# A fused two-layer kernel: how the Sinkhorn scaling starts and returns to logarithms, and where the last residual sums stand

## The chip, the cores and the metric

The kernel runs on one core of a Trainium2 chip. A core has five engines that run side by side and meet through semaphores: TensorE (PE: matrix products and transposes), VectorE (DVE), ScalarE (ACT: functions from tables), GpSimd (POOL) and SyncE (SP: starts most transfers). The metric is the device time of one execution in microseconds (us), lower is better.

## The reference, cut to what matters

Two layers work on x of 2 x 512 x 512. The change touches only the end of the second layer: the attention's residual sum, the layer norm after it, and the last block, in which each of the 1024 tokens has its own 4 x 4 matrix, made doubly stochastic by 50 scaling steps.

```python
x = x + ga * _L1_attn_ref(h, ...)
h = _layernorm(x, axis=-1) * (1 + cb) + sb
# last block, on h as x
x_norm = x * jax.lax.rsqrt(jnp.mean(x * x, axis=-1, keepdims=True) + RMS_EPS)
H_res_logits = (x_norm @ W_res.T).reshape(B, T, n, n) + H_res_base
Z = logits / tau                        # tau 0.1
def step(carry, _):                     # 50 times, u and v from zero
    u, v = carry
    u = -jax.nn.logsumexp(Z + v[..., None, :], axis=-1)
    v = -jax.nn.logsumexp(Z + u[..., :, None], axis=-2)
    return ((u, v), None)
H_res = jnp.exp(Z + u[..., :, None] + v[..., None, :])
H_pre = jax.nn.softmax(H_pre_logits, axis=-1)
H_post = jax.nn.softmax(H_post_logits, axis=-1)
H_res = (1.0 - g) * I + g * H_res
x_pre = jnp.einsum('btnc,btn->btc', x_streams, H_pre)
y = x_pre @ W_branch
x_mixed = jnp.einsum('btij,btjc->btic', H_res, x_streams)
y_distributed = jnp.einsum('btc,btn->btnc', y, H_post)
```

## The kernel before, in words

Every engine runs one straight program. `story` calls stages in one order for all five engines, and a stage adds instructions only to the engines whose class defines it; so the order on each engine is the order of the calls, and an engine that waits holds everything behind it. The 1024 tokens are eight tiles of 128 rows: tiles 0 to 3 are batch 0, tiles 4 to 7 batch 1. `acc[:, i]` holds x of tile i, `hh[b][:, i % 4]` its attention output and later its normed row.

`attentions` runs 16 rounds (Q), eight to a batch, each over four key tiles (kt): `scores_b` (PE, then exponentials on ACT), `pv` (PE), `out1` (ACT copies the sums) and `out2` (PE turns them, DVE divides and writes 2 x 32 columns of `hh`). `out2` of a round is called at kt 1 of the next one; that of the last round stands behind the loop. PSUM banks 4, 5 and 6 are taken in turn (`spin`), so a product can wait until an older one is read.

`head(E, b)` then takes the four tiles of a batch: `residual` (DVE multiplies `hh` by the modulation row `mt[1, 2, b]`, POOL adds it to `acc`), `moments` (DVE statistics, POOL power), `norm` (ACT), `scaled_rows` (DVE multiplies, POOL adds), `square` (ACT), `turn_l` (PE transposes, ACT copies), `rms`, and `logits` (PE, then DVE). Batch 0's head is spread over the second batch's rounds; batch 1's stands alone behind the loop, with a product `logits` of a tile ahead of the next tile's transposes.

`mix_y(1)` makes the two softmaxes of batch 1. Then `sinkhorn` works on all tiles at once, 128 columns a step. W holds logarithms, P = exp(W), T a scaled copy, m the sums, a and b their reciprocals. It takes maximum, difference, exponential, sum, logarithm and difference once along rows and once along columns, which is one of the 50 steps, and then 49 steps in blocks of 17, 16 and 16. A step is six DVE instructions: multiply by b, row sums, reciprocal a, multiply by a, column sums, reciprocal b; the first of a block has no multiply by b. Between blocks logarithms of a and b are added to W and P is made anew ("return to logarithms"). Beside it, `merged` puts `branch` (the product with W_branch) on ACT, POOL and PE, one of its pieces for each three or four calls of the scaling. `finish` mixes, and SP writes the output.

Lines used below: L1082 and L1700 residual, L1087 to L1092 and L1705 moments, L1442 norm, L1099 and L1713 scaled rows, L792 transposes, L803 logits product, L1225 its result, L1231 to L1273 scaling on DVE, L1563 exponential, L1568 logarithm, L1284 to L1288 softmax sums.

## Time and profile before

| | us |
|---|---|
| median of 3 runs | 1542.0 |
| lowest and highest | 1539.73 and 1542.78 |
| the profiled execution | 1540.01 |
| its span, first to last instruction | 1538.2 |

The profile is one execution, and durations come from it; 1.81 us of it lie around its span. Of the span PE is busy 82%, DVE 65%, POOL 48% and ACT 41%, but the last 185 us are another kernel than the rest: there PE has little to do and DVE most.

### The profile page before, as it was taken

What the parts mean: (1) busy time and instruction counts of PE and PEld (TensorE: products, weight loads), DVE (VectorE), ACT (ScalarE), POOL (GpSimd) and SP (SyncE); (2) the same over time, 40 slices, a digit from 0 to 9 for tenths busy, and PEclk for the clock granted to TensorE, in tenths of its full rate; (3) what the DMA queues carried; (4) which work ended last, traced back from release to release, by engine and by line L of the source; (5) the groups of instructions that cost most, each with busy time, mean ns of one, the idle gap of its engine ahead of it and who ended that gap; (6) DMA issues with size and microseconds to landing.
All of it is one profiled execution on the core that took longest, in us unless ns stands there. A gap on an engine that the chain in (4) does not pass through costs nothing. (4 is left out here: it accounts for less than half of the span.)

```text
span 1538.2 us, 18571 instructions
## 1 busy us (share of the span) xinstructions
PE 1260.4 (82%) x6079; PEld 890.4 (58%) x6079; DVE 1001.4 (65%) x1717; ACT 630.0 (41%) x1177; POOL 736.3 (48%) x742
## 2 busy tenths in 40 slices
PE   4889999999999999999999999777989999841000
PEld 2677767767767777777777777556843334330000
DVE  6836655656565666656556566675678887447888
ACT  2334333333433333333334333246227767733223
POOL 0456765665756656657657657665200011041007
PEclk9999999999999999999999999898959989955555
DMA  4211122122122112112112111210754200000001
GB/s 157 79 49 55 56 69 83 55 62 89 40 79 69 56 56 67 56 56 69 55 56 69 53 58 49 80 58 1 144 113 69 53 30 2 1 1 0 0 0 55
DMA packets 70552, 86.47 MB, mean 56 GB/s; under 512 B 6853, under 2 KB 40805, under 8 KB 69882
## 3 DMA queue, kind: packets, MB, share of 16 engines
q1 hardware_dynamic: 68586, 82.57, 19.8%
q10 hardware_dynamic: 1872, 2.72, 0.5%
q8 instruction: 50, 0.82, 0.2%
q14 instruction: 44, 0.36, 0.1%
HBM read 77.49 MB, written 7.51 MB: 55 GB/s over the span
## 5 line engine op out<-in xcount | busy, mean ns | idle before, releaser
L1183 DVE TENSOR_REDUCE nm<-banks 128x2 f32<-128x1024 f32 x128 | 152.2, 1221 | 33.4 <-PE banks L742 32.9
L1425 ACT ACTIVATE yTh<-yF 128x512 fp32r<-128x512 f32 x64 | 40.4, 632 | 318.9 <-DVE yF L1035 318.9
L1637 POOL TENSOR_TENSOR sw<-sw,sinT 128x512 f32<-128x512 f32 x80 | 103.3, 1291 | 137.8 <-ACT sw L1376 137.8
L1651 POOL TENSOR_TENSOR dec<-gb,gcol 128x512 f32<-128x512 f32 x64 | 70.8, 1107 | 195.3 <-DVE Sd L1001 191.2
L1531 ACT ACTIVATE Pb<-banks 128x512 f32<-128x512 f32 x256 | 135.0, 602 | 52.8 <-PE banks L763 52.4
L540 PE MATMUL banks<-hTh,wgh 128*128 128x512 f32 x256 | 122.1, 477 | 0.0
L973 DVE SCALAR_TENSOR_TENSOR gs<-tg,banks 128x512 f32<-128x512 f32 x64 | 44.0, 688 | 118.4 <-ACT tg L1383 118.4
L592 PE MATMUL banks<-st,qt 128*128 128x128 f32 x384 | 80.7, 294 | 37.1 <-DVE Sd L1001 21.1
L620 PE MATMUL banks<-woh,yTh 128*128 128x512 f32 x256 | 104.6, 409 | 3.5 <-DVE yTl L1038 3.5
L540 PE MATMUL banks<-hTh,wqh 128*128 128x512 f32 x256 | 106.3, 415 | 0.0
L620 PE MATMUL banks<-woh,yTl 128*128 128x512 f32 x256 | 101.7, 397 | 0.0
L620 PE MATMUL banks<-wol,yTh 128*128 128x512 f32 x256 | 101.0, 394 | 0.0
L540 PE MATMUL banks<-hTh,wql 128*128 128x512 f32 x256 | 100.7, 394 | 0.0
L540 PE MATMUL banks<-hTh,wgl 128*128 128x512 f32 x256 | 100.7, 393 | 0.0
L540 PE MATMUL banks<-hTl,wgh 128*128 128x512 f32 x256 | 100.7, 393 | 0.0
L540 PE MATMUL banks<-hTl,wqh 128*128 128x512 f32 x256 | 99.9, 390 | 0.0
L1700 POOL TENSOR_TENSOR acc<-acc,hh 128x512 f32<-128x512 f32 x8 | 10.5, 1313 | 184.3 <-DVE hh L1082 184.3
L763 PE MATMUL banks<-qsT,ksT 50*128 50x512 f32 x256 | 92.9, 503 | 7.1 <-DVE hh L1207 4.5
L1038 DVE TENSOR_TENSOR yTl<-yF,yTh 128x512 fp32r<-128x512 f32 x64 | 68.7, 1073 | 44.7 <-ACT yTh L1425 44.7
L593 PE MATMUL banks<-xc,Sd 128*128 128x128 f32 x512 | 95.9, 286 | 0.0
L592 PEld LDWEIGHTS banks<-st,qt 128*128 128x128 f32 x384 | 64.9, 205 | 46.2 <-DVE Sd L1001 24.4
L1642 POOL TENSOR_TENSOR qT<-tt,sw 128x512 f32<-128x512 f32 x64 | 83.1, 1298 | 14.6 <-DVE tt L968 6.5
(307 smaller groups left out, 3378.3 us busy)
## 6 DMA issues: line engine op xcount, KB each, us to landing
gb<-g_scr SPq DMA_DIRECT2D x64, 256.0 KB, 3.3
raw<-in_wmod SPq DMA_DIRECT2D x40, 256.0 KB, 2.7
raw<-in_wg SPq DMA_DIRECT2D x32, 256.0 KB, 2.7
raw<-in_wo SPq DMA_DIRECT2D x32, 256.0 KB, 2.8
raw<-in_wq SPq DMA_DIRECT2D x30, 256.0 KB, 2.6
qsT<-q_scr SPq DMA_DIRECT2D x24, 256.0 KB, 6.6
q_scr<-hl SPq DMA_DIRECT2D x32, 128.0 KB, 4.3
mt<-mods_scr SPq DMA_DIRECT2D x12, 256.0 KB, 4.8
```

The lines of the kernel that those rows point to most:

```text
L540: mm = pe.matmul(banks[bk][:, :], w_[:, k, :], x_[:, k, b * 512:(b + 1) * 512], start=(c == 0), stop=(c == 11))
L592: pe.matmul(o, qt[:, h, :], st[:, h, :], start=True, stop=False)
L593: mm = pe.matmul(o, Sd[:, h, :], xc[:, h, :], start=(n == 0), stop=True)
L620: mm = pe.matmul(banks[bO][:, :], y_[:, h, :], w_[:, :], start=(c == 0), stop=(c == 11))
L763: pe.matmul(banks[bk], k_[64 * g:64 * g + 50, p // 4, kt * 128:(kt + 1) * 128], q_[64 * g:64 * g + 50, p % 8, :], start=True, stop=True).t ...
L973: ve.scalar_tensor_tensor(out=gs[t % 2][:, n, :], in0=tg[:, :], scalar=1.0, in1=banks[bk][:, :], op0=ALU.add, op1=ALU.mult).then_inc(*v_ga ...
L1038: ve.tensor_tensor(yTl[:, :, :], yF[:, :, :], yTh[:, :, :].bitcast(F32), ALU.subtract).then_inc(*v_yl.up(s))
L1183: ve.tensor_reduce(nm[:, b, i, p:32:16], pairs[z_][:, :].rearrange("p (g t) -> p g t", g=2), AX.X, ALU.max, negate=True).then_inc(*v_nm.up ...
L1531: ac.activation(Pb[kt % 2][:, 2 * g + pr, :], banks[bk], ACTF.Exp, scale=0.25).then_inc(*a_exp.up(b, qd, kt, pr, g))
L1637: po.tensor_tensor(s_[:, :], s_[:, :], sinT[:, :], ALU.mult).then_inc(*g_rope.up("sin", kind, t, n))
L1642: po.tensor_tensor(dst, tt1[j][:, :], s_[:, :], ALU.add).then_inc(*g_rope.up("add", kind, t, n))
L1651: po.tensor_tensor(dec[:, :, :], gb[s % 2][:, :, :], bc(gcol[:, t % 2, heads(t), n], 2, 128), ALU.subtract).then_inc(*g_dec.up("sub", s))
```

## The change

It has three parts.

1. The scaling begins from W with the rows' and then the columns' maxima taken off, with no logarithm. T = exp of W without row maxima gives the first row sums, P = exp of W without both gives all that follows. 25 steps, one return to logarithms, 25 steps. The step's order is unchanged.
2. The softmaxes of batch 1 (`mix_y`, in two parts) stand inside the return, and the branch of batch 0 runs beside the first half, that of batch 1 beside the second.
3. In the last round `out2` of the round before is called at kt 0 instead of kt 1, and columns 0 to 223 of each half of tiles 4 to 7 are multiplied (DVE) and added (POOL) there (`residual_most`). Behind the loop only 2 x 32 columns a tile are left, done for all four tiles by two DVE instructions (`residual_last`). `last_head` replaces the head of batch 1: all moments, then all scaled rows (the additions of tiles 5 and 7 on DVE), then squares and transposes, with a tile's transposes ahead of the product of the tile before.

```diff
+    def most(t):
+        return t.rearrange("p (g c) -> p g c", g=2)[:, :, 0:224]
+    def last(t):
+        return t.rearrange("p i (g c) -> p i g c", g=2)[:, :, :, 224:256]
...
+        def residual_most(self, i):
+            ve, b = self.e, i // 4
+            h_ = most(hh[b][:, i % 4, :])
+            ve.wait_ge(*v_out("o", b, 6))
+            ve.wait_ge(*d_mt[2, b](1))
+            ve.tensor_tensor(h_, h_, most(mt[1, 2, b][:, :]), ALU.mult).then_inc(*v_res.up("most", i))
+        def residual_last(self, b):
+            ve, a_, h_ = self.e, last(acc[:, 4 * b:4 * b + 4, :]), last(hh[b][:, :, :])
+            m_ = mt[1, 2, b][:, :].rearrange("p (g c) -> p g c", g=2)[:, :, 224:256]
+            ve.wait_ge(*v_out("o", b, 7))
+            ve.tensor_tensor(h_, h_, bc(m_, 1, 4), ALU.mult).then_inc(*v_res.up("last", b))
+            ve.wait_ge(*v_res("last", b))
+            ve.tensor_tensor(a_, a_, h_, ALU.add).then_inc(*v_res.up("sum", b))
...
         def moments(self, of, i):
             ve = self.e
+            if of == "h" and i >= 4:
+                ve.wait_ge(*v_res("sum", 1))
             ve.wait_ge(*g_x(of, i))
...
+            if i in (5, 7):
+                ve.wait_ge(*v_ln("h", "c", i))
+                ve.wait_ge(*d_mt[3, b](1))
+                ve.tensor_tensor(h_, h_, mt[1, 3, b][:, :], ALU.add).then_inc(*v_ln.up("h", "d", i))
...
+        def residual_most(self, i):
+            po, b = self.e, i // 4
+            a_ = most(acc[:, i, :])
+            po.wait_ge(*v_res("most", i))
+            po.tensor_tensor(a_, a_, most(hh[b][:, i % 4, :]), ALU.add).then_inc(*g_x.up("h", i))
...
+    def last_head(E):
+        E.residual_last(1)
+        for i in range(4, 8):
+            E.moments("h", i), E.norm("h", i)
+        for i in range(4, 8):
+            E.scaled_rows(i)
+        for i in range(4, 8):
+            E.square(i)
+            E.turn_l(i, E.spin())
+            E.rms(i)
+            if i > 4:
+                E.logits(i - 1, E.spin())
+        E.logits(7, E.spin())
...
-    def sinkhorn(E):
...
+    def scaling_steps(E, c, k, n, first):
+        for it in range(n):
+            if it:
+                E.sk_mul(c, k + 1, c.T, c.bv, True), (yield)
+                E.sk_sum(c, k + 2, c.T, False, v_sk("sk", k + 1)), (yield)
+                E.sk_inv(c, k + 3, c.av), (yield)
+                k += 3
+            E.sk_mul(c, k + 1, c.T, c.av, False, None if it else first), (yield)
+            E.sk_sum(c, k + 2, c.T, True, v_sk("sk", k + 1)), (yield)
+            E.sk_inv(c, k + 3, c.bv), (yield)
+            k += 3
+    def first_half(E):
+        c = Sink
+        E.sk_scale(c, 0), (yield)
+        E.sk_max(c, 1, False, v_sk("sk", 0)), (yield)
+        E.sk_sub(c, 2, False), (yield)
+        E.sk_exp(c, 3, c.T), (yield)
+        E.sk_max(c, 4, True, v_sk("sk", 2)), (yield)
+        E.sk_sub(c, 5, True, 3), (yield)
+        E.sk_exp(c, 6, c.P), (yield)
+        E.sk_sum(c, 7, c.T, False, a_sk("sk", 3), v_sk("sk", 5)), (yield)
+        E.sk_inv(c, 8, c.av), (yield)
+        yield from scaling_steps(E, c, 8, 25, 6)
+        k = KMID
+        E.sk_ln(c, k + 1, c.av, v_sk("sk", k - 2)), (yield)
+        E.sk_ln(c, k + 2, c.bv, v_sk("sk", k)), (yield)
+        E.mix_y(1, 0)
+        E.sk_add(c, k + 3, c.av, False, a_sk("sk", k + 1)), (yield)
+        E.sk_add(c, k + 4, c.bv, True, v_sk("sk", k + 3), a_sk("sk", k + 2)), (yield)
+        E.sk_exp(c, k + 5, c.P), E.mix_y(1, 1), (yield)
+    def second_half(E):
+        c, k = Sink, KMID + 5
+        E.sk_sum(c, k + 1, c.P, False, a_sk("sk", k)), (yield)
+        E.sk_inv(c, k + 2, c.av), (yield)
+        yield from scaling_steps(E, c, k + 2, 25, None)
+        for part in range(3):
+            E.sk_h(c, k + 2 + 3 * 49 + 1 + part, part), (yield)
...
-                if kt == 1 and Q:
+                if kt == (1 if Q < 15 else 0) and Q:
                     E.out2(*before(b, qd), E.spin())
+                if Q == 15 and kt < 2:
+                    E.residual_most(4 + 2 * kt), E.residual_most(5 + 2 * kt)
...
-        stream(E, head, 1).rest()
-        E.mix_y(1)
-        merged(stream(E, sinkhorn), joined(stream(E, branch, 0), stream(E, branch, 1))).rest()
+        last_head(E)
+        merged(stream(E, first_half), stream(E, branch, 0)).rest()
+        merged(stream(E, second_half), stream(E, branch, 1)).rest()
```

Three places show how instructions stand. First PE, from the last round's products of probabilities and values (Pb) to the logits products (rwt); `cst,oS` is out2, `cst,hh` the transposes. Before:

```order
L783 MATMUL banks<-cst,oS 128x128 x4
L763 MATMUL banks<-qsT_218,ksT_212 128x512 x4
L773 MATMUL banks<-Pb_243,vp_214 32x512 x4
L773 MATMUL banks<-Pb_244,vp_214 32x512 x4
L783 MATMUL banks<-cst,oS 128x128 x4
L792 MATMUL banks<-cst,hh_166 128x128 x4
L803 MATMUL banks<-rwt,hT_248 128x24 x4
L792 MATMUL banks<-cst,hh_166 128x128 x4
L803 MATMUL banks<-rwt,hT_248 128x24 x4
L792 MATMUL banks<-cst,hh_166 128x128 x4
```

After, in the same place:

```order
L794 MATMUL banks<-cst,oS 128x128 x4
L774 MATMUL banks<-qsT_218,ksT_212 128x512 x4
L784 MATMUL banks<-Pb_244,vp_214 32x512 x4
L774 MATMUL banks<-qsT_218,ksT_212 128x512 x4
L784 MATMUL banks<-Pb_243,vp_214 32x512 x4
L784 MATMUL banks<-Pb_244,vp_214 32x512 x4
L794 MATMUL banks<-cst,oS 128x128 x4
L803 MATMUL banks<-cst,hh_166 128x128 x8
L814 MATMUL banks<-rwt,hT_248 128x24 x4
L803 MATMUL banks<-cst,hh_166 128x128 x4
L814 MATMUL banks<-rwt,hT_248 128x24 x4
L803 MATMUL banks<-cst,hh_166 128x128 x4
```

The first out2 moved one group of scores and one of values up, and two tiles' transposes now stand ahead of the first logits product.

Second DVE, from the out2 of the last round (`rd` and `hh<-banks,rd`) on. Before:

```order
L1203 RECIPROCAL rd<-banks 128x16
L1207 TENSOR_TENSOR hh_166<-banks,rd 128x4x32 x2
L1082 TENSOR_TENSOR hh_166<-hh_166,mt_253 128x512 x2
L1087 BN_STATS bst<-acc 128x6
L1089 BN_AGGR mv<-bst 128x2
L1091 TENSOR_SCALAR nmean<-mv 128x1
L1092 TENSOR_SCALAR ve<-mv 128x1
L1082 TENSOR_TENSOR hh_166<-hh_166,mt_253 128x512
```

After, from one out2 earlier:

```order
L1235 RECIPROCAL rd<-banks 128x16
L1239 TENSOR_TENSOR hh_166<-banks,rd 128x4x32 x2
L1100 TENSOR_TENSOR hh_166<-hh_166,mt_253 128x2x224 x4
L1235 RECIPROCAL rd<-banks 128x16
L1239 TENSOR_TENSOR hh_166<-banks,rd 128x4x32 x2
L1106 TENSOR_TENSOR hh_166<-hh_166,mt_253 128x8x32
L1108 TENSOR_TENSOR acc<-acc,hh_166 128x8x32
L1115 BN_STATS bst<-acc 128x6
L1117 BN_AGGR mv<-bst 128x2
L1119 TENSOR_SCALAR nmean<-mv 128x1
L1120 TENSOR_SCALAR ve<-mv 128x1
```

Four multiplications went ahead of the last out2, and two of 256 columns stand between it and the first statistics.

Third ACT, at a return to logarithms: the logarithms of a and b, the exponential P, table loads, and pieces of the branch (`yb`, `prod`). The first return before:

```order
L1568 ACT_TABLE_LOAD
L1568 ACTIVATE a<-a 128x32
L1604 ACTIVATE banks<-yb_270,hp 128x128
L1568 ACTIVATE b<-b 128x32
L1563 ACT_TABLE_LOAD
L1563 ACTIVATE P<-W 128x128
```

The only return after:

```order
L1608 ACT_TABLE_LOAD
L1608 ACTIVATE a<-a 128x32
L1608 ACTIVATE b<-b 128x32
L1646 ACTIVATE mx_264<-yb_272,hp 128x128
L1615 ACT_TABLE_LOAD
L1615 ACTIVATE hp<-hp 128x32
L1603 ACTIVATE P<-W 128x128
```

The softmax exponential (hp) came in ahead of P. From the end of attention on, ACT's program held eight table loads, and now holds these two.

## Rows read from the trace of the kernel before

**Rows 1.** Busy time by stage: stretch, length, busy us (instructions) per engine, clock, DMA.

```profile
1353.30:1365.10 11.80, 0.00 (x0) 0.00 (x0) 10.28 (x25) 2.44 (x3) 9.90 (x12) 0.57 0.01 1
1365.10:1381.80 16.70, 11.48 (x48) 9.76 (x48) 3.21 (x11) 5.76 (x13) 7.41 (x9) 0.50 0.00 1
...
1391.60:1500.00 108.40, 7.35 (x23) 4.83 (x23) 95.15 (x291) 27.93 (x86) 8.59 (x14) 0.50 0.00 0
```

**Rows 2.** Timeline, end of attention: start, us, engine, line, [idle before <- releaser].

```profile
1348.30 0.26 DVE L1203 RECIPROCAL rd<-banks 128x16 f32<-128x16 f32 x1 [11.85 <-PE banks L783]
...
1354.14 1.29 DVE L1082 TENSOR_TENSOR hh<-hh,mt 128x512 f32<-128x512 f32 x2
...
1356.59 0.69 DVE L1087 BATCH_NORM_STATS2 bst<-acc 128x6 f32<-128x512 f32 x1 [1.15 <-POOL acc L1700]
```

**Rows 3.** Timeline, head of batch 1: moments, norm, scaled rows.

```profile
1358.26 0.69 DVE L1087 BATCH_NORM_STATS2 bst<-acc 128x6 f32<-128x512 f32 x1
...
1359.27 0.14 DVE L1092 TENSOR_SCALAR ve<-mv 128x1 f32<-128x1 f32 x1
...
1360.20 0.99 POOL L1705 TENSOR_TENSOR rs<-ve,neghalf 128x1 f32<-128x1 f32 x1
...
1361.49 0.81 ACT L1442 ACTIVATE hh<-acc,nmr,rs 128x512 f32<-128x512 f32 x1 [1.62 <-POOL nmr L1707]
...
1363.84 1.26 POOL L1713 TENSOR_TENSOR hh<-hh,mt 128x512 f32<-128x512 f32 x1
```

**Rows 4.** Timeline, transposes and logits products of batch 1.

```profile
1365.15 1.12 PE L792 MATMUL banks<-cst,hh 128*128 128x128 f32 x4 [11.87 <-POOL hh L1713]
...
1372.64 1.90 PE L803 MATMUL banks<-rwt,hT 128*128 128x24 f32 x8 [0.69 <-ACT hT L1558]
...
1374.37 1.09 PE L792 MATMUL banks<-cst,hh 128*128 128x128 f32 x4
...
1379.66 1.90 PE L803 MATMUL banks<-rwt,hT 128*128 128x24 f32 x8 [0.69 <-ACT hT L1558]
1381.60 0.24 DVE L1225 SCALAR_TENSOR_TENSOR lg<-banks,r,rbc 128x24 f32<-128x24 f32 x1 [3.20 <-PE banks L803]
```

**Rows 5.** Timeline, from the softmax sums to the first block of scaling.

```profile
1382.58 0.19 DVE L1284 TENSOR_REDUCE hs<-hp 128x8 f32<-128x32 f32 x1 [0.30 <-ACT hp L1573]
...
1383.15 0.22 DVE L1231 TENSOR_SCALAR W<-lg 128x128 f32<-128x128 f32 x1
...
1384.05 0.31 ACT L1563 ACTIVATE T<-W 128x128 f32<-128x128 f32 x1 [1.21 <-DVE W L1246]
...
1386.50 1.28 ACT L1563 ACT_TABLE_LOAD   x1
...
1387.80 0.31 ACT L1563 ACTIVATE T<-W 128x128 f32<-128x128 f32 x1
...
1391.59 0.29 DVE L1241 TENSOR_REDUCE m<-P 128x32 f32<-128x128 f32 x1 [1.33 <-ACT P L1563]
```

**Rows 6.** Timeline, the two returns to logarithms.

```profile
1428.36 0.23 ACT L1568 ACTIVATE a<-a 128x32 f32<-128x32 f32 x1 [23.48 <-DVE b L1251]
...
1430.65 0.28 DVE L1241 TENSOR_REDUCE m<-P 128x32 f32<-128x128 f32 x1 [1.00 <-ACT P L1563]
...
1465.06 0.23 ACT L1568 ACTIVATE a<-a 128x32 f32<-128x32 f32 x1 [22.58 <-DVE b L1251]
...
1467.36 0.29 DVE L1241 TENSOR_REDUCE m<-P 128x32 f32<-128x128 f32 x1 [1.29 <-ACT P L1563]
```

**Rows 7.** Groups on DVE, 1391.6 to 1501.7: count | busy, mean ns | idle before.

```profile
L1241 DVE TENSOR_REDUCE m<-T 128x32 f32<-128x128 f32 x95 | 31.5, 332 | 3.2
...
L1256 DVE TENSOR_TENSOR T<-P,a 128x128 f32<-128x128 f32 x49 | 14.6, 298 | 1.7
```

**Rows 8.** Busy time in two stretches of the last round, columns as in Rows 1.

```profile
1346.00:1348.00 2.00, 2.00 (x12) 0.71 (x4) 0.00 (x0) 0.07 (x1) 0.00 (x0) 0.50 0.00 0
1348.00:1350.00 2.00, 1.55 (x10) 0.71 (x12) 0.75 (x3) 1.27 (x3) 0.00 (x0) 0.95 0.00 0
```

91 lines of the change are left out of this document (38 added, 53 removed).

## The prediction

> **What bounds the kernel now.** I read the busy time by stage first, then the timeline of the last 185 us, because the change leaves all before the last attention round as it is. The reader is to see a serial tail. From 1353.3 to 1365.1 DVE and POOL work in turn and PE does nothing; from 1365.1 to 1381.8 PE works at the low clock; from 1391.6 to 1500 DVE is busy 95.15 of 108.4 us [rows 1], and what is not busy there are the gaps between dependent small instructions and the two returns. So each us taken off this chain is a us of the kernel, as long as the replacement is on the same chain. `finish`, behind it, is the same code and starts when the scaled matrix H is there.
>
> **Part 1, residual sums beside the last round.** DVE has been idle for 11.85 us when it divides the second last round's sums [rows 2], so four multiplications of 448 columns fit. A 512-column one takes 0.65 us (1.29 for two) [rows 2], so about 0.6 each, 2.4 in all; POOL's additions, of which the 512-column kind takes 1.26 [rows 3], are at most 1.26 each, 5.0 in all. Even taken strictly one after another that is 7.4 us. They can start when the moved out2 has been divided, which I put some 4 us ahead of 1348.30, the time of its division now [rows 2], since it moves one key tile up and then waits for nothing that is late. They end at about 1352, ahead of the last out2's DVE work (up to 1354.14) [rows 2]. So they cost nothing; without that cover they would cost what they cost now. Moving out2 from kt 1 to kt 0 moves four transposes and one wait for a bank from one key tile to the one before; the sum of PE's work in the round stays, and I take 0, with bounds of -1 and +1 us, as the idle of ACT and PE around out2 may split otherwise.
>
> Now the first multiplication starts at 1354.14 and the first statistics at 1356.59, waiting for POOL [rows 2]: 2.45 us. After, two DVE instructions of 256 columns stand there. Between 0.29 us for 128 columns [rows 5] and 0.65 for 512, that is 0.42 each, with gaps 0.9. First statistics at 1355.05.
>
> **Part 2, moments and scaled rows.** A tile's moments take 1359.27 - 1358.26 plus 0.06, 1.07 us [rows 3]; the four now run back to back: the fourth is ready at 1359.3. POOL's power to ACT's norm is 1360.20 to 1361.49, 1.29 us from the power's start, which is 0.2 behind the DVE result, and powers follow each other each 1.2. Powers then start at 1356.3, 1357.5, 1358.7 and 1359.9, POOL is through at about 1361.1, and the norms start at 1357.5 to 1361.15 and take 0.81 each [rows 3]. DVE multiplies tile 4's row from 1359.35, well ahead of POOL. **POOL's first scaled row** can only start when its four powers are done, at 1361.1; with the 0.4 us that DVE may hold it up, and 1.26 for itself [rows 3], tile 4 is ready at 1362.75 where it now is at 1365.1 (the first transposes start at 1365.15 [rows 4]). Tile 5 needs no POOL and is ready by 1361.5 to 1362.7. Tiles 6 and 7, with POOL and DVE in turn, are ready at 1365.2 and 1365.8.
>
> **Part 3, transposes and logits.** Now a tile costs 3.51 us ((1379.66 - 1372.64) / 2 [rows 4]): product 1.90, transposes that end 0.92 behind the product's end (1374.37 + 1.09 - 1372.64 - 1.90), then the copy on ACT, for which PE waits. With the next tile's transposes ahead of the product that wait is covered. After, PE does T4 1.12, T5 0.94, L4 1.90, T6 0.94, L5 1.90, T7 0.94, L6 1.90, L7, and the result starts 1.94 behind L7's start (1381.60 - 1379.66 [rows 4]): 11.6 us. T6 is due at 1366.7 and T7 at 1369.6, behind their rows, so nothing else is late. The last logits come at 1362.75 + 11.6 = 1374.3 instead of 1381.60. **Parts 1 to 3 give 7.3 us.**
>
> **Part 4, the start of the scaling.** Now from the last logits (1381.60) to the first sum of P (1391.59) it is 9.99 us [rows 5]: the softmax of batch 1, then two rounds of exponential and logarithm with four table loads of 1.28 in DVE's way. After, 0.27 to the scale as the softmax has it now, scale 0.25, maximum, difference, maximum, difference at 0.33 to 0.37 each (reductions 0.332 + 3.2 / 95 = 0.366, 128-column products 0.298 + 1.7 / 49 = 0.333 [rows 7]), and the first sum starts 1.9 us behind the last logits. The exponential T (0.31, start 0.9 behind the scale [rows 5]) is done before the second difference asks for it, P is done before the first multiply. Saved: 8.1.
>
> **Part 5, the steps.** Sixteen steps less one multiply take 1465.06 - 1430.65 = 34.41 us [rows 6]; with 0.33 for the multiply a step is (34.41 + 0.33) / 16 = 2.17. There were 49 in three blocks and are 50 in two: one step more and one left-out multiply fewer, 2.5 us lost. The branch brings the same POOL instructions as before, so the same disturbance is in the step.
>
> **Part 6, the return.** Now 1428.36 to 1430.65 and 1465.06 to 1467.36, 2.29 and 2.30 [rows 6]. After, the logarithm of a runs beside the last sum and reciprocal. Behind the reciprocal of b: logarithm of b, one branch piece on ACT (starts at 0.12, ends at 0.51), the table load 1.28, the softmax's exponential at 1.80, P right behind it, done at 2.27. DVE fits the softmax's difference and both additions into the load. But it has the softmax's sums, reciprocal and product in front of the next sum: they start at 2.06 and take 0.57 (1383.15 - 1382.58 [rows 5]). So 2.63, once. Saved: 4.59 - 2.63 = 2.0. If the softmax did not wait, it would be 2.3.
>
> A load and the exponential behind it start 1.30 us apart (1386.50 to 1387.80 [rows 5]), so a switch costs here the load and nothing more. The Trainium skill (ScalarE: Activation LUTs, What ACT_TABLE_LOAD costs) adds a drain of about 1.38 us to a load of 1.28; the trace doesn't show it. By the page the return would be some 1.4 longer.
>
> **The sum.** 7.3 + 8.08 - 2.5 + 1.96 = 14.8. The profiled execution took 1540.01 us, and would take 1525.2. It is 2.0 us under the median of the runs shown, 1542.0, near the lowest; so against the median, which is what I forecast, 1542.0 - 14.8 = **1527.2**.
>
> **Rivals.** (a) **PE's clock comes back in the head.** The granted clock is 0.50, the 1.2 GHz level, from 1365.1 to 1381.8, with PE busy 11.48 of 16.7 us [rows 1]. In the last round it was at 0.50 with PE busy 2.00 of 2.00 and at 0.95 in the next 2 us [rows 8]. After, PE works nearly without a break for 11 us. If the clock rose some 4 us in, the remaining 7.6 us would halve at most, 3.8, but ACT's copies then bind: I take 3, so 1524.2. Against it: the stage before it leaves PE idle for 9 us, and it starts low. The Trainium skill (TensorE: Matmul & The Clock Gate, Part 1) says that activity releases the throttle, and so speaks for this rival; what the stage shows so far, the low clock at two thirds busy, does not decide it. Chance 0.2.
>
> (b) **The head saves less.** POOL now runs four powers before any scaled row, and DVE and POOL take turns on their two-input instructions. If rows 4, 6 and 7 come each one POOL instruction and a DVE one later than I worked out (1.26 + 0.65), and the residual sums of the last round end 1 us late, 3 us are lost: 1530.2. For it: the bst row waited 1.15 us for POOL [rows 2]. Against: the four additions have 6 us of room. Chance 0.13.
>
> (c) **Slower: the step gets longer.** 298 small instructions decide the scaling. If the branch, which ACT can now run through at once instead of stopping at logarithms (it waited 23.48 and 22.58 us there [rows 6]), pressed POOL's instructions into DVE's, each step would pay. From 14.8 / 50 = 0.3 us a step on, the kernel is no faster; at 0.4 it is 5 us slower, 1547. For it, only that a product shows 0.298 mean where an undisturbed one is 0.29 [rows 7]. Against it: POOL has 14 instructions in 108 us, 8.59 us busy [rows 1]; even if each stopped DVE for its whole length it were 8.6. Chance 0.03.
>
> (d) **The last round pays what was moved into it**: out2 at kt 0 holds back the scores by a bank, or the DVE products delay the last out2. If the round ends later by what the residuals took, 2.4 us and more, the time is 1530. It is the case in which the change does not do what it says. Chance 0.06.
>
> **How the numbers follow.** My forecast has 0.5, (a) 0.2, (b) 0.13, (c) 0.03, (d) 0.06, and 0.08 is for a gain a little larger or smaller by causes not named. The forecast's own spread is the 1 us of part 1, 1 us of the head and the 1.5 us that the runs differ by. The range reaches down to (a) with 2 us of room and up past (b): 1522 to 1531.5. What a measurement can tell is about 0.2%, 3 us. Faster by more than that holds in all but (c): 0.96; within it 0.02; slower 0.02.
>
> **What would show it.** The four products of 2 x 224 columns and POOL's four additions all before the last out2, with DVE idle after; the first statistics 1.4 us behind the last `hh` product; first transposes 9 us, not 12, behind the last out2; L to L each 2.84 us at 0.50; the last logits 7.3 us nearer to the last out2; first sum of T 1.9 us behind them; the return 2.6 us; 50 steps of 2.17. The stretch behind the last `hh` product would be 14.8 us shorter, `finish` as long as now. Wrong would be: a clock of 1.00 in the head, POOL's first scaled row later than 8 us behind the last out2, or a step over 2.2.

## The result and the profile after

The changed kernel takes 1520.87 us (median of 4 runs, 1519.26 to 1522.55), the kernel before beside it 1540.87 (4 runs, 1538.23 to 1542.78): a ratio of 0.9872, 95% interval 0.9852 to 0.9891. That is 20.0 us less where 14.8 were forecast, and 1.1 us below the range. The profiled execution took 1520.73, its span is 1518.9.

First the busy time by stage of the kernel after (stretch, length, then busy us and instructions of PE, weight load, DVE, ACT, POOL, then the granted clock, DMA share and GB/s): from the second last to the last division of sums, from there to the first transposes, the head up to the last logits, and the two halves of the scaling. The third row answers to the row of before from 1365.10 on [rows 1].

```profile
1342.75:1350.37 7.62, 5.97 (x36) 1.81 (x36) 4.88 (x8) 4.73 (x9) 5.51 (x4) 1.00 0.00 0
1350.37:1359.01 8.64, 0.01 (x1) 0.01 (x1) 8.19 (x24) 3.28 (x5) 4.54 (x9) 0.69 0.01 2
1359.01:1369.36 10.35, 10.31 (x48) 9.95 (x48) 4.30 (x12) 5.21 (x13) 3.78 (x5) 0.50 0.01 2
1371.36:1425.80 54.44, 3.92 (x12) 2.50 (x12) 49.35 (x150) 12.26 (x41) 4.72 (x8) 0.50 0.00 0
1428.46:1482.42 53.96, 3.91 (x12) 2.50 (x12) 48.84 (x150) 11.53 (x40) 4.79 (x8) 0.50 0.00 0
```

PE now works through the head without a break, 10.31 of 10.35 us, where it was busy 11.48 of 16.70, and its clock stays at 0.50.

Cutting both traces at the same events gives the balance. The second last and last divisions (L1203 before, L1235 after), first statistics, first transposes, last logits (L1225, L1257), the first sum of the loop and the first product of the finish (H) are starts of instructions:

| stage | before | after | difference | forecast |
|---|---|---|---|---|
| start of the program to the third last division | 1335.67 | 1334.26 | -1.41 | 0 |
| two rounds' divisions, third last to last | 17.66 | 16.11 | -1.55 | 0 |
| last division to first statistics | 3.26 | 1.73 | -1.53 | -1.54 |
| to the first transposes | 8.56 | 6.91 | -1.65 | -0.9 |
| to the last logits | 16.45 | 10.35 | -6.10 | -4.9 |
| to the first product of H | 120.07 | 113.06 | -7.01 | -7.54 |
| to the end | 36.53 | 36.48 | -0.05 | 0 |
| sum | 1538.2 | 1518.9 | -19.3 | -14.8 |

The third row and those below it, with the second, are the changed part: 17.9 us. The first row is code that the change does not touch.

The end of attention and the head on DVE, kernel after (start, us, engine, line, instruction, in brackets the idle time before and what ended it); it answers to [rows 2] and [rows 3]:

```profile
1342.75 0.26 DVE L1235 RECIPROCAL rd<-banks 128x16 f32<-128x16 f32 x1 [7.71 <-PE banks L794]
...
1343.57 4.13 DVE L1100 TENSOR_TENSOR hh<-hh,mt 128x448 f32<-128x448 f32 x4
1350.37 0.26 DVE L1235 RECIPROCAL rd<-banks 128x16 f32<-128x16 f32 x1 [2.67 <-PE banks L794]
...
1351.18 0.42 DVE L1106 TENSOR_TENSOR hh<-hh,mt 128x256 f32<-128x256 f32 x1
1351.64 0.42 DVE L1108 TENSOR_TENSOR acc<-acc,hh 128x256 f32<-128x256 f32 x1
1352.10 0.69 DVE L1115 BATCH_NORM_STATS2 bst<-acc 128x6 f32<-128x512 f32 x1
...
1357.70 1.80 DVE L1131 TENSOR_TENSOR hh<-hh,mt 128x512 f32<-128x512 f32 x1
```

The four moved multiplications end at 1347.70 and DVE then waits 2.67 us for PE, so they cost nothing. POOL in the same kernel:

```profile
1344.27 5.51 POOL L1748 TENSOR_TENSOR acc<-acc,hh 128x448 f32<-128x448 f32 x4 [36.11 <-DVE hh L1100]
1353.34 0.55 POOL L1753 TENSOR_TENSOR rs<-ve,neghalf 128x1 f32<-128x1 f32 x1 [3.56 <-DVE ve L1120]
...
1356.54 0.93 POOL L1753 TENSOR_TENSOR rs<-ve,neghalf 128x1 f32<-128x1 f32 x1 [0.25 <-DVE ve L1120]
...
1357.69 1.26 POOL L1763 TENSOR_TENSOR hh<-hh,mt 128x512 f32<-128x512 f32 x1
```

Its additions end at 1349.78, 0.6 us before the last division. Three of the four powers take 0.55 us and not 0.99, and the first scaled row ends at 1358.95; the transposes start 0.06 later. PE in the head, which answers to [rows 4]:

```profile
1359.01 1.97 PE L803 MATMUL banks<-cst,hh 128*128 128x128 f32 x8 [8.67 <-POOL hh L1763]
1360.81 1.90 PE L814 MATMUL banks<-rwt,hT 128*128 128x24 f32 x8
1362.53 1.09 PE L803 MATMUL banks<-cst,hh 128*128 128x128 f32 x4
1363.42 1.74 PE L814 MATMUL banks<-rwt,hT 128*128 128x24 f32 x8
1364.99 1.09 PE L803 MATMUL banks<-cst,hh 128*128 128x128 f32 x4
1365.87 3.45 PE L814 MATMUL banks<-rwt,hT 128*128 128x24 f32 x16
```

No row but the first has a wait in brackets; before, the first product waited 2.86 us for ACT's copy and each of the other three 0.69. The start of the scaling and the one return, DVE and ACT, which answer to [rows 5] and [rows 6]:

```profile
1369.36 0.24 DVE L1257 SCALAR_TENSOR_TENSOR lg<-banks,r,rbc 128x24 f32<-128x24 f32 x1 [1.46 <-PE banks L814]
...
1371.36 0.29 DVE L1274 TENSOR_REDUCE m<-T 128x32 f32<-128x128 f32 x1
...
1425.80 0.23 ACT L1608 ACTIVATE b<-b 128x32 f32<-128x32 f32 x1 [0.57 <-DVE b L1286]
...
1426.34 1.28 ACT L1615 ACT_TABLE_LOAD   x1
1427.63 0.23 ACT L1615 ACTIVATE hp<-hp 128x32 f32<-128x32 f32 x1
...
1427.89 0.19 DVE L1324 TENSOR_REDUCE hs<-hp 128x8 f32<-128x32 f32 x1 [1.33 <-ACT hp L1615]
...
1428.46 0.28 DVE L1274 TENSOR_REDUCE m<-P 128x32 f32<-128x128 f32 x1
```

The first sum comes 2.00 us behind the last logits (1.9 forecast), the return takes 2.66 (2.63 forecast), and DVE's only wait in it is 1.33 us for the exponential behind the table load.

### The profile page after: what moved, and what is told of

Its sections match the earlier page's. It is cut to its first block and busy times, and to the rows that moved or that the text cites. A ratio compares the mean times of both kernels' runs of the same rounds, so it can differ in the third digit from the quotient of the medians.

```text
span 1518.9 us, 18570 instructions
## 1 busy us (share of the span) xinstructions
PE 1256.9 (83%) x6079; PEld 888.5 (58%) x6079; DVE 1006.9 (66%) x1722; ACT 621.5 (41%) x1165; POOL 732.3 (48%) x740
## 5 line engine op out<-in xcount | busy, mean ns | idle before, releaser
L979 DVE TENSOR_TENSOR tt<-banks,cosT 128x512 f32<-128x512 f32 x80 | 55.3, 691 | 53.1 <-ACT sw L1416 52.3
```

## The experiments

The theories: the gain is a sum of separate pieces on one serial chain (last round, head, start of the scaling, return), each of a size that can be read by undoing it alone. Against it stood that the last round's 1.55 us and the 1.41 us ahead of it were chance of the clock, that the head's surplus came from somewhere else than POOL and PE, and that a piece pays back elsewhere. "After" means the changed kernel. Stage lengths are cut as in the table above. Where a kernel was run once, only the stage lengths of its trace are read, not its time: wherever kernels share the code of a stage, these lengths agree within 0.05 us up to the first product of H.

### The two halves of the change

**before_again**: the kernel before, unchanged, as a measure of what a comparison can tell.

> The kernel before, unchanged, timed and profiled once more as a control. What it tells is how far two executions of the same program stand apart. Theory A (the low-clock stretch in the last attention round, 1344.8 to 1349 in the trace of before, is a property of the old order of that round): it is there again, the last round (division of out2 of the second last round to that of the last) takes 17.6 us, and the time is 1540.9. Rival B (the clock's low stretches fall where they fall, different in each execution): the last round takes 16.1 or 17.6 by chance, the list of low stretches differs from that of the first trace in one or two entries of some 4 us, each worth 1.4 to 1.6 us, and the runs spread over 3 to 4 us.

Measured: 1538.38 us (10 runs) beside 1538.54 (19 runs), ratio 1.0006 (0.9991 to 1.0021). Its two rounds take 17.68, head 28.27, last logits to H 120.04, each within 0.03 of the first trace. Its third last division is at 1332.99, 2.7 us earlier than in the first trace of the same code: the part ahead of the last rounds is where executions differ.

**scaling_only**: the new scaling behind the old last round and head.

```diff
-        last_head(E)
+        stream(E, head, 1).rest()
...
-                if kt == (1 if Q < 15 else 0) and Q:
+                if kt == 1 and Q:
-                if Q == 15 and kt < 2:
-                    E.residual_most(4 + 2 * kt), E.residual_most(5 + 2 * kt)
```

> Only the scaling part of the change (start with maxima, one return, softmax of batch 1 in it, branches split over the two halves); last round and head as before. From the two traces the scaling part is worth 8.0 (start) + 1.9 (return) - 2.9 (steps) = 7.0 us: 1533.9. If the parts were not additive, because the head's end meets the branch differently, it would be 1 us or more away. Under rival B the last round shows 16.1 or 17.6 us by chance, under theory A 17.6.

Measured: 1532.84 us, ratio 0.9953 (0.9936 to 0.9971), 5.7 us by the medians. Two rounds 17.64, head 28.29, last logits to H 113.04. The scaling's 7.0 us of the trace are there without the rest.

**head_only**: the new last round and head in front of the old scaling (49 steps behind the logarithms, softmaxes ahead).

```diff
-        merged(stream(E, first_half), stream(E, branch, 0)).rest()
-        merged(stream(E, second_half), stream(E, branch, 1)).rest()
+        E.mix_y(1, 0), E.mix_y(1, 1)
+        merged(stream(E, sinkhorn), joined(stream(E, branch, 0), stream(E, branch, 1))).rest()
```

> Only the head part of the change (out2 earlier in the last round, residual sums beside it, new head of batch 1); scaling with two returns and its old start. Head stage (last out2's division to the last logits) 19.0 us instead of 28.3: 9.3 gained, against 7.3 in the prediction. Theory A: 9.3 + 1.55 = 10.9 gained, 1530.0, last round 16.1 us. Rival B: 9.3 gained on average, 1531.6, last round 16.1 or 17.6. Rival C (the extra 2 us of the head came only with the new scaling behind it): 1533.6.

Measured: 1528.81 us, ratio 0.9935 (0.9913 to 0.9956). Two rounds 16.12, head 18.98, last logits to H 120.05. 9.7 us by the medians, 10.85 by the trace. With scaling_only the stages add up to 17.9 us, the changed part's whole gain: the halves do not disturb one another.

### The last round

**out2_late**: out2 stays at kt 1, the moved residual sums at kt 1 and 2.

```diff
-                if kt == (1 if Q < 15 else 0) and Q:
+                if kt == 1 and Q:
                     E.out2(*before(b, qd), E.spin())
-                if Q == 15 and kt < 2:
-                    E.residual_most(4 + 2 * kt), E.residual_most(5 + 2 * kt)
+                if Q == 15 and kt in (1, 2):
+                    E.residual_most(2 + 2 * kt), E.residual_most(3 + 2 * kt)
```

> The changed kernel, but out2 of the second last round stays at kt 1, and the residual products and sums follow at kt 1 and 2 instead of 0 and 1. The four sums then end some 2 to 3 us later, at about the time of the last out2's division; tile 4 and 5 are there, tiles 6 and 7 are asked for 2 and 3 us later. Theory A: the last round has its low-clock stretch again and takes 17.6 us, and the time is 1522.4 to 1523. Rival B: no difference beyond 0.5 us, 1521. If POOL's sums came too late, the head stage would be longer than 19.0 by up to 2 us.

Measured: 1524.20 us, ratio 0.9908 (0.9886 to 0.9930). Two rounds 17.67, as in the kernel before, and the head 19.80 instead of 18.99. DVE of out2_late:

```profile
1348.08 4.12 DVE L1100 TENSOR_TENSOR hh<-hh,mt 128x448 f32<-128x448 f32 x4
1352.29 0.26 DVE L1235 RECIPROCAL rd<-banks 128x16 f32<-128x16 f32 x1
...
1353.56 1.23 DVE L1108 TENSOR_TENSOR acc<-acc,hh 128x256 f32<-128x256 f32 x1
```

Now the multiplications end just ahead of the last division, POOL's four additions (5.73 us from 1348.78) run to 1354.51, and the addition of 256 columns on DVE takes 1.23 us instead of 0.42: that is the head's 0.8. The round's 1.56 us are apart from it.

**out2_alone** and **out2_alone_again**: the kernel before with nothing but the call moved.

```diff
-                if kt == 1 and Q:
+                if kt == (1 if Q < 15 else 0) and Q:
                     E.out2(*before(b, qd), E.spin())
```

> The kernel before with one call moved: in the last round out2 stands at kt 0 instead of 1; no residual sums in the round, old head, old scaling. If out2's place alone keeps the clock up in the last round, the two divisions around it add up to 16.1 us instead of 17.7 and no low stretch lies in the round: 1.5 us under before. If the residual products beside it were needed, or the new head, it is 17.6 to 17.7 with the low stretch, and the time is that of before. The head stage is the old one, 28.3 us, either way.

> The kernel before with one call moved (in the last round out2 at kt 0 instead of 1), once more for its trace: nine timed executions of it gave 1536.7 to 1541.1 us where before gave 1535.9 to 1542.7 beside it, which decides nothing on 1.5 us. Theory A (out2's place alone keeps the clock up): no low stretch in the last round, the two divisions around it add up to 16.1 us. Rival: the stretch is there as in before and it is 17.7; then the products and additions beside the round, or what they hold up, keep it away in the changed kernel.

Measured: out2_alone 1538.06 us, ratio 0.9998 (0.9985 to 1.0010), that is from 2.3 us less to 1.5 us more. The execution of it that was profiled took 2580.27 us, so its stages can't be set beside the others'. out2_alone_again took 1539.02 beside 1539.09, and its trace has two rounds of 16.11, head 28.27, last logits to H 120.03. So the call alone makes the round 1.55 us shorter; a timing of this size can neither show nor exclude it. PE, first of the kernel before:

```profile
1344.65 0.70 PE L763 MATMUL banks<-qsT,ksT 50*128 50x512 f32 x1 [0.45 <-ACT Pb L1531]
1345.28 1.93 PE L773 MATMUL banks<-Pb,vp 128*32 128x512 f32 x8
1347.15 1.12 PE L783 MATMUL banks<-cst,oS 128*128 128x128 f32 x4
```

and of out2_alone_again, where the same kinds of products stand at other times:

```profile
1343.09 1.06 PE L773 MATMUL banks<-Pb,vp 128*32 128x512 f32 x8
1344.09 0.66 PE L783 MATMUL banks<-cst,oS 128*128 128x128 f32 x4
...
1348.46 0.50 PE L763 MATMUL banks<-qsT,ksT 50*128 50x512 f32 x1 [0.45 <-ACT Pb L1531]
```

Eight products of probabilities and values 1.93 against 1.06, out2's transposes 1.12 against 0.66, a score 0.70 against 0.50: 1.53 us together, the 1.55 of the round. The granted clock says why. Kernel before, then out2_alone_again, 4 us each, from 9.3 and 9.0 us behind the third last division:

```profile
1345.00:1349.00 4.00, 3.69 (x15) 1.10 (x14) 0.66 (x3) 1.34 (x4) 0.00 (x0) 0.60 0.00 0
```
```profile
1345.29:1349.29 4.00, 3.22 (x18) 1.16 (x22) 0.27 (x2) 3.47 (x8) 0.00 (x0) 1.00 0.00 0
```

0.60 and 1.00. The kernel before has a stretch at 0.50 that begins 9.1 us behind the third last division, in both of its traces (1344.8 to 1348.2, and 1342.1 to 1345.5), and so have scaling_only (1350.1 to 1353.5) and out2_late (1343.7 to 1347.1). None of the twelve traces with the call at kt 0 has it, and all twelve have two rounds of 16.1.

**out2_later**: the call at kt 2, residual sums at kt 2 and 3.

```diff
-                if kt == (1 if Q < 15 else 0) and Q:
+                if kt == (1 if Q < 15 else 2) and Q:
...
-                if Q == 15 and kt < 2:
-                    E.residual_most(4 + 2 * kt), E.residual_most(5 + 2 * kt)
+                if Q == 15 and kt > 1:
+                    E.residual_most(2 * kt), E.residual_most(1 + 2 * kt)
```

> The changed kernel with the last round's out2 at kt 2, and the residual products and sums at kt 2 and 3. If each later place is as bad as kt 1, the low stretch is there and the last round takes 17.7 us; if kt 1 is only an unlucky place, the stretch is away and it takes 16.1. Beside that POOL's four sums end some 3 us later than in out2_late, behind the last out2: the head stage, 19.8 there, would be 22 to 23.

Measured (one run): 1530.40 us; two rounds 21.53 and head 19.90, where 17.7 or 16.1 and 22 to 23 were expected. A stretch of its last round, then DVE and PE at its end:

```profile
1350.00:1352.00 2.00, 1.74 (x6) 0.49 (x9) 0.00 (x0) 1.97 (x4) 0.00 (x0) 0.50 0.00 0
```
```profile
1355.10 4.10 DVE L1100 TENSOR_TENSOR hh<-hh,mt 128x448 f32<-128x448 f32 x4
...
1356.83 1.12 PE L794 MATMUL banks<-cst,oS 128*128 128x128 f32 x4 [0.72 <-ACT oS L1578]
...
1359.13 0.25 DVE L1235 RECIPROCAL rd<-banks 128x16 f32<-128x16 f32 x1
```

The low clock now lasts from 1346.7 to the end of the round, and the two rounds take 5.4 us more than after. Not all of that is the clock. Out2's division starts 1.16 us behind its transposes at the low clock (1353.13 to 1354.29 for the out2 before it), which for the last one would be 1357.99; it starts at 1359.13, because DVE is on the moved multiplications (1355.10 to 1359.20). So some 1.1 us belong to the multiplications and some 4.3 to the clock: the place of four transposes within a round of equal work decides between 16.1, 17.7 and about 20.4 us.

Why the clock falls in the one order and not in the other is not settled by these runs. In two stretches of 2 us, from 5.1 to 1.1 us ahead of the fall, PE was busy 1.83 and 1.63 us in the kernel before and 1.83 and 1.62 in out2_alone_again, and ACT alike. The last 1.1 us are where they part, kernel before, then out2_alone_again:

```profile
1343.70:1344.80 1.10, 0.65 (x4) 0.21 (x2) 0.00 (x0) 0.80 (x2) 0.00 (x0) 0.99 0.00 0
```
```profile
1344.30:1345.40 1.10, 0.88 (x6) 0.39 (x4) 0.58 (x3) 0.19 (x1) 0.00 (x0) 1.00 0.00 0
```

In the second, out2's transposes stand there. All five traces with a fall have PE busy 0.65 of these 1.1 us, all twelve without have 0.88 or 0.89. That goes with the fall; no run varies this alone, so it is not shown to be its cause.

### Inside the head

**product_first**: a tile's product ahead of the next tile's transposes, as before.

```diff
             E.square(i)
+            if i > 4:
+                E.logits(i - 1, E.spin())
             E.turn_l(i, E.spin())
             E.rms(i)
-            if i > 4:
-                E.logits(i - 1, E.spin())
```

> The changed kernel with the old order of products in the head alone: a tile's logits product ahead of the next tile's transposes. Head stage split: division to first statistics 1.73, statistics to first transposes 6.9, as in the trace of after. First transposes to last logits: 16.4 us as before (10.4 in after), if the order alone is worth the 6.1 us; 12 to 14 if a part of it came from rows being ready earlier. The forecast priced that order at 4.9 us (16.45 against 11.6).

Measured (one run): 1525.95 us; first transposes as after (+6.89 behind the statistics), from there to the last logits 14.27 instead of 10.35, head 22.90. PE of product_first:

```profile
1365.60 1.90 PE L814 MATMUL banks<-rwt,hT 128*128 128x24 f32 x8 [0.69 <-ACT hT L1598]
1367.33 1.09 PE L803 MATMUL banks<-cst,hh 128*128 128x128 f32 x4
1369.11 1.90 PE L814 MATMUL banks<-rwt,hT 128*128 128x24 f32 x8 [0.69 <-ACT hT L1598]
```

The old pitch of 3.51 us a tile is back, with the old wait. The order on PE alone is worth 3.9 us, of the head's 9.3 the largest piece. The other 2.2 of this stage's 6.1 us came with the rows of the tiles: the first product waited 2.86 us for its copy before, and 0.69 here.

**rows_on_pool**: all four additions of the scaled rows on POOL.

```diff
-            if i in (5, 7):
-                ve.wait_ge(*v_ln("h", "c", i))
-                ve.wait_ge(*d_mt[3, b](1))
-                ve.tensor_tensor(h_, h_, mt[1, 3, b][:, :], ALU.add).then_inc(*v_ln.up("h", "d", i))
```

> The changed kernel with all four additions of the scaled rows on POOL, as before. If POOL's additions bind: four of 1.26 plus waits behind DVE, tile 7's row some 1.5 to 2.5 us later than in after (1361.8 to 1362.4 there), still ahead of the time at which PE asks for it (1365). Then nothing is lost: head 19.0 to 19.3. If the move to DVE was what made the head faster than forecast, the head is 20 to 21 us.

Measured (one run): 1523.36 us; first transposes +7.35 (after: +6.91), to the last logits 10.97, head 20.05. The division of the additions between two engines is worth 1.06 us.

**sums_behind**: all residual sums behind the last round again, `residual` of tiles 4 to 7 in a row, the rest of the new head kept.

```diff
-        E.residual_last(1)
+        for i in range(4, 8):
+            E.residual("h", i)
...
-                if Q == 15 and kt < 2:
-                    E.residual_most(4 + 2 * kt), E.residual_most(5 + 2 * kt)
```

> The changed kernel without residual sums in the last round: out2 stays early, but all four 512-column products and additions stand behind the last out2. DVE does four products (2.6 to 4 us), POOL four additions of 1.26 in a row, tile 4's first. Statistics start 3.2 us behind the division as before instead of 1.73, and each of the next ones waits for POOL (1.3 each instead of 1.07), and POOL's powers stand behind the additions: first transposes some 3.5 us later than in after, head 22 to 23 us. By theory A the last round keeps the high clock (16.1 us from division to division), since only out2's place decides; if the products in it did, it is 17.6.

Measured (one run): 1529.65 us; two rounds 16.10, so the round is as short without the sums in it as with them: they are truly hidden. First statistics +5.37 instead of +1.73, first transposes +8.05, head 23.78. The hidden sums are worth 4.8 us in this head, three times the 1.5 us by which the first statistics came sooner than in the kernel before: there the sums stood between one tile's moments and the next, here all four would stand ahead of the first.

### The start of the scaling and the return

**no_return**: 50 steps in a row from the same start, with the softmaxes ahead of the scaling, where they used to stand.

```diff
         yield from scaling_steps(E, c, 8, 25, 6)
-        k = KMID
-        E.sk_ln(c, k + 1, c.av, v_sk("sk", k - 2)), (yield)
-        E.sk_ln(c, k + 2, c.bv, v_sk("sk", k)), (yield)
-        E.mix_y(1, 0)
-        E.sk_add(c, k + 3, c.av, False, a_sk("sk", k + 1)), (yield)
-        E.sk_add(c, k + 4, c.bv, True, v_sk("sk", k + 3), a_sk("sk", k + 2)), (yield)
-        E.sk_exp(c, k + 5, c.P), E.mix_y(1, 1), (yield)
...
+        E.mix_y(1, 0), E.mix_y(1, 1)
```

> The changed kernel with no return to logarithms at all: 50 steps in a row, the softmax of batch 1 ahead of the scaling as before the change. The result has the same definition, only a and b span more. From last logits to H: 113.06 less 2.66 (the return) plus 0.33 (one multiply by b) plus 1.2 (the softmax back on DVE's way, 1.28 from its first to its last instruction before) less 0: 111.9. If table load and logarithms had not been on the way, it would be 113.1 or more.

**softmax_ahead**: the return kept, the softmaxes ahead of the scaling.

```diff
-        E.mix_y(1, 0)
...
-        E.sk_exp(c, k + 5, c.P), E.mix_y(1, 1), (yield)
+        E.sk_exp(c, k + 5, c.P), (yield)
...
+        E.mix_y(1, 0), E.mix_y(1, 1)
```

> The changed kernel with the softmax of batch 1 back ahead of the scaling and the one return kept. Start: last logits to first sum 3.27 instead of 2.00. Return: without the softmax's exponential and its three DVE instructions behind the load, the first sum stands behind P alone: 2.66 becomes 2.27 (load, then P at 1.80, read at 2.13), or 2.1. So last logits to H 113.06 + 1.27 - 0.4 to 0.55 = 113.8 to 113.9. If the return hid the softmax wholly, it would be 114.3.

Measured (one run each): no_return 1522.15 us, last logits to H 111.77, so without the return H comes 1.29 us sooner than in after; softmax_ahead 1526.27, 113.59, which is 0.2 to 0.3 under what was expected; after 113.06. ACT and DVE of softmax_ahead at its return:

```profile
1432.04 0.23 ACT L1608 ACTIVATE b<-b 128x32 f32<-128x32 f32 x1 [0.57 <-DVE b L1286]
...
1434.21 0.28 DVE L1274 TENSOR_REDUCE m<-P 128x32 f32<-128x128 f32 x1 [1.55 <-ACT P L1603]
```

The bare return is 2.17 us and spares one multiply of 0.33, 1.84 net; the difference of the two kernels, 113.59 - 111.77 = 1.82, says the same. Putting the softmaxes into it makes it 0.49 longer and the start 1.26 shorter (first sum 3.26 behind the last logits in both kernels, 2.00 after), which should give 0.77; last logits to H gives 0.53. The rest is in the steps and was not followed. The prediction's aside that the return would be 2.3 without the softmax was 0.13 too long.

### What binds the head next

**after_again**: the changed kernel once more, as a neighbour for early_rows.

> The changed kernel, unchanged, as a control beside the next two. If the clock's dip in the last round goes with out2's old place, its last round is 16.1 us without a low stretch again, head 19.0, last logits to H 113.1, and the time is 20 us under before on the same chip, give or take 1.5 us by the low stretches ahead of the last round, which differ from one execution to the next.

Measured: 1522.01 us (4 runs) beside 1539.65 (7 runs), ratio 0.9884 (0.9866 to 0.9902); two rounds 16.11, head 18.99, last logits to H 113.07. Its third last division stands at 1335.80, so here the untouched part ahead is 0.13 us later than in the first trace of before, not 1.41 earlier. The interval holds the 17.9 us of the changed part (0.9884 x 1539.65 is 17.9 less).

**early_rows**: additions of tiles 4 and 5 on DVE (those of 6 and 7 on POOL), and both rows ahead of tile 7's moments, so that the first transposes no longer wait for POOL's four powers and its scaled row.

```diff
-            if i in (5, 7):
+            if i in (4, 5):
...
-        for i in range(4, 8):
+        for i in range(4, 7):
             E.moments("h", i), E.norm("h", i)
-        for i in range(4, 8):
-            E.scaled_rows(i)
+        E.scaled_rows(4), E.scaled_rows(5)
+        E.moments("h", 7), E.norm("h", 7)
+        E.scaled_rows(6), E.scaled_rows(7)
```

> The changed kernel with one more step in the head: tiles 4 and 5 are scaled whole on DVE (product and addition) ahead of tile 7's moments, tiles 6 and 7 have their addition on POOL. By the trace of after, tile 4's row waits 2.7 us for POOL to get through four powers. If that wait is what starts the transposes, they start 2.0 to 2.4 us earlier (4.6 us behind the first statistics instead of 6.9); the wait for tile 6 gives back up to 1 us, so the head is 17.5 to 18 us and the time 1 to 1.5 us under the changed kernel. If the head were bound by PE's own chain from the statistics on, no change.

Measured: 1524.44 us, ratio 0.9899 (0.9881 to 0.9916). The transposes start 2.24 us earlier (+4.67), but the last logits come 14.16 behind them: head 20.56, 1.6 more than after where 1 to 1.5 less was expected. PE and ACT of early_rows:

```profile
1357.71 1.11 PE L803 MATMUL banks<-cst,hh 128*128 128x128 f32 x4 [6.44 <-DVE hh L1131]
...
1363.32 1.90 PE L814 MATMUL banks<-rwt,hT 128*128 128x24 f32 x8 [3.17 <-ACT hT L1598]
```
```profile
1361.36 0.81 ACT L1482 ACTIVATE hh<-acc,nmr,rs 128x512 f32<-128x512 f32 x1 [2.81 <-POOL nmr L1755]
...
1362.69 0.57 ACT L1598 ACTIVATE hT<-banks 128x512 f32<-128x512 f32 x1
```

ACT waited 2.81 us for tile 7's power, with square and copy of tile 4 queued behind the wait. A wait had taken the place of the one removed. A kernel with this head and 50 steps in a row (early_no_return) gave no result; early_head_no_return below takes its place.

**early_head**: additions of tiles 4, 5 and 7 on DVE, the rows of tiles 4 to 6 ahead of tile 7's moments, and tile 7's norm on ACT behind the copies of tiles 4 and 5.

```diff
-            if i in (5, 7):
+            if i in (4, 5, 7):
...
-        for i in range(4, 8):
+        for i in range(4, 7):
             E.moments("h", i), E.norm("h", i)
-        for i in range(4, 8):
+        for i in range(4, 7):
             E.scaled_rows(i)
+        E.moments("h", 7)
...
+            if i == 5:
+                E.norm("h", 7)
+                E.scaled_rows(7)
```

> The changed kernel; in the head tiles 4, 5 and 6 are normed and multiplied ahead of tile 7's moments, the additions of 4, 5 and 7 are on DVE, and ACT's norm of tile 7 stands behind the squares and copies of tiles 4 and 5. In early_rows first transposes came 2.24 us earlier, but ACT waited with the norm of tile 7 in front of the copy for the first product, and the head was 1.57 us longer. If that wait was the whole loss, the first product now starts some 8.7 us behind the last out2's division (10.4 in after), its end is 8.55 behind that, and the head is 17.3 to 17.6 instead of 19.0. If PE or DVE bind otherwise, it is 19 or more.

**early_head_no_return**: early_head with 50 steps in a row, the softmaxes' parts around the first row sums of the 26th step.

```diff
...
+        E.mix_y(1, 0)
+        E.sk_mul(c, k + 1, c.T, c.bv, True), (yield)
+        E.sk_sum(c, k + 2, c.T, False, v_sk("sk", k + 1)), (yield)
+        E.sk_inv(c, k + 3, c.av), E.mix_y(1, 1), (yield)
```

> early_head and no return to logarithms (50 steps in a row), the softmax of batch 1 in two parts among the first instructions of the second 25 steps. From the last logits to H 111.77 - 1.27 + 1.0 = 111.5. With a head of 17.3 to 17.6: 3.0 to 3.3 us under the changed kernel, 1518 to 1519 where the changed one is at 1522.

Measured: early_head 1520.63 us, ratio 0.9872 (0.9850 to 0.9894); first transposes +4.68, last logits 10.74 behind them, head 17.15, 1.84 us under after's. early_head_no_return 1518.29 us (1516.44 to 1520.43), ratio 0.9860 (0.9839 to 0.9882); head 17.16, last logits to H 111.92. PE of early_head:

```profile
1359.69 1.11 PE L803 MATMUL banks<-cst,hh 128*128 128x128 f32 x4 [6.44 <-DVE hh L1131]
...
1361.92 1.74 PE L814 MATMUL banks<-rwt,hT 128*128 128x24 f32 x8
```

The wait of 3.17 us in front of the first product is gone. early_head_no_return has the lowest median of all, and by its stages it saves 1.83 + 1.14 = 3.0 us more than the change; its interval overlaps that of after_again, so the timings alone don't separate the two.

## Why the prediction was right or wrong, point by point

**Last round, taken as 0 with bounds of 1 us: wrong, the step that failed most.** It is -1.55 us in the trace. The prediction reckoned with equal work for PE and with idle time that might split otherwise, and overlooked that the round already contained a low stretch of the clock, though [rows 8] showed it: those rows were read for rival (a) and not for the round's own price. out2_alone_again shows that the call's place alone takes the stretch away, out2_late that all the rest of the change leaves it there. That the moved sums cost nothing was right (sums_behind: 16.10 without them, 16.11 with), though not by the room that was reckoned: the four multiplications took 4.13 us and not 2.4, POOL's additions 5.51 and not at most 5.0, and they ended 0.6 us before the last division. Rival (d) did not come; out2_later, where the multiplications meet the last division and hold it some 1.1 us, shows that it was a real one.

**First statistics: right.** 1.73 us behind the last division; the working gives 1.72. The 256-column instructions took the 0.42 worked out.

**Moments and rows: right in kind, 0.8 too long.** The first transposes came 8.64 us behind the last division, not 9.42. The power was priced at 0.99 from a row in which it ran beside a two-input instruction of DVE; between one-input statistics it takes 0.55, and only the fourth, which meets DVE's multiplication, takes 0.93. So the powers kept the moments' pitch of 1.07 instead of 1.2, and the hold-up of 0.4 for POOL's first row did not occur.

**Transposes and logits: right in kind, 1.2 too long.** 10.35 us, not 11.6. The order worked as described, without a wait of PE. But the three products with PE's work behind them were priced at 1.90, the duration from start to last result, and the transposes at 0.94 to 1.12. By the starts in after, these products hand over after 1.72, 1.57 and 1.57 and the transposes after 0.89 to 0.90; that makes the 1.2. Distances between starts were wanted. For the product [rows 4] had one, 1.73 from its start at 1372.64 to the transposes at 1374.37; from transposes to product PE waited in between.

**Start of the scaling: 8.08 forecast, 7.99 measured.** **Return: 1.96 forecast, 1.93 measured** (4.59 to 2.66). What binds it is the table load: a load and the exponential behind it start 1.29 us apart (1426.34 and 1427.63). By this the trace does not show the drain of 1.38 us that the Trainium skill (ScalarE: Activation LUTs, What ACT_TABLE_LOAD costs) adds to each load; by an estimate with that drain the return would have been 4.0.

**The steps: 2.5 lost forecast, 2.9 measured** (105.49 to 108.40 us outside the returns). The 25 steps of the first half take (54.44 + 0.33) / 25 = 2.19, of the second 2.17. That is far from rival (c), 0.3 us a step. Neither this nor another of the signs named as wrong appeared: the clock in the head was 0.50, POOL's first scaled row started 7.3 us behind the last out2's division. The term that failed most stood among none of them.

**The clock in the head, rival (a): did not come.** The granted clock was 0.50, the 1.2 GHz level, through 10.35 us in which PE was busy 10.31. The Trainium skill (TensorE: Matmul & The Clock Gate, Part 1) says that activity releases the throttle; this trace does not show a release in that stretch.

**The sum.** In the changed part 14.8 were forecast and 17.9 measured: 1.55 for the round, 1.98 for the head, 0.05 at the end, less 0.53 in the scaling (0.09 at the start, 0.03 in the return, 0.41 in the steps). Of the 6.3 us between 1527.2 and 1520.87 these are 3.05. Another 1.1 is that the median of before moved from 1542.0 to 1540.87 with a fourth run. The last 2.1 lie outside the stages of the change and within the noise: the interval is 16.8 to 22.8 us. 1.41 of them stand in the two traces ahead of it. There before has a low stretch of the clock, 218.4 to 221.8, that after lacks, and across it after goes from 0.1 us behind before to 1.5 ahead. The same place in after and in after_again:

```profile
219.00:222.00 3.00, 3.00 (x20) 2.40 (x20) 2.23 (x4) 2.79 (x5) 2.19 (x3) 1.00 0.24 79
```
```profile
219.00:222.00 3.00, 3.00 (x16) 3.00 (x16) 2.05 (x3) 1.81 (x3) 2.19 (x3) 0.50 0.29 85
```

after and after_again are the same program, at 1.00 and 0.50; and before_again, the same program as before, has 1.00. This one comes and goes between executions, unlike the one in the last round.

So the 1.1 us by which the time fell below the range are not the round's alone: without the 2.1 us outside the change it would have been inside. The range was too narrow at its lower end because the head and the last round were each given 1 us, one term was priced by durations where pitches were meant, and no allowance was made for the untouched 1335 us, which in the profiled executions of all kernels end between 1332.99 and 1340.90.

## What to carry to other kernels

Price a chain on one engine by the distance between starts, taken where the engine does not wait, and a small instruction by what its neighbour engine does beside it: both errors here made the forecast too long. When four tiles go through one serial head, put a tile's transposes ahead of the product before it (3.9 us here) and check what each in-order engine has queued behind its next wait (early_head, with tile 7's norm moved on ACT, tile 6's row ahead of tile 7's moments and one addition more on DVE, is 3.4 us shorter than early_rows). Where a round has a stretch at the low clock, moving one short call can remove it or make it longer, so read the granted clock of the round before calling such a move free.

## What the runs showed of the hardware

The low stretch in the last round belongs to the program's order, not to the execution: five traces of five with the call at kt 1 or 2 have it, none of twelve with it at kt 0 has, for the same total work of PE. What PE did differently ahead of the fall is 0.65 us of work in 1.1 us against 0.88. Other low stretches, such as that at 219 us, differ between executions of one program.

A power of 128x1 on POOL takes 0.55 us while DVE runs statistics and 0.93 to 1.00 beside a multiplication with two inputs (after, before, sums_behind). DVE suffers the same way: the addition of a scaled row (L1131) takes 1.80 us in after beside POOL's scaled row. In early_head POOL has only its 128x1 power and the 128x1 product behind it while DVE adds tile 4's row, and the same instruction takes 0.69:

```profile
1358.94 0.69 DVE L1131 TENSOR_TENSOR hh<-hh,mt 128x512 f32<-128x512 f32 x1
```
